# Second attention of a two-layer network: score matmuls in two 64-row halves of TensorE, and a new order of work

## The reference

```
x   = layernorm(features)             # context, 512 rows per batch
lat = layernorm(latents)              # the residual stream, 512 rows per batch
q   = (lat @ Wq) per head * SCALE     # 16 heads of width 64
kv_input = concatenate([x, lat])      # 1024 keys per batch
k, v = kv_input @ Wk, kv_input @ Wv   # per head
sim = q k^T
sim = sim - max(sim, axis=-1)         # over all 1024 keys, masked ones too
sim = where(kv_mask, sim, -inf)
out = softmax(sim) v
return out @ Wo
```

## Time and profile before

| | us |
|---|---|
| median of 3 runs (3788.44 to 3791.84) | 3791.21 |
| the profiled execution | 3788.78 |
| its span, first to last instruction | 3787.2 |

### The profile page before, as it was taken

The page is one execution under the profiler, slowest core; times in us unless marked ns, Lnnn a source line. Parts: engine busy times, 40 slices in busy tenths (PEclk is TensorE's granted clock), DMA queues, the critical chain, the costliest instruction groups (busy, mean ns, idle before and its releaser), DMA issues. The chain is left out here.

```text
span 3787.2 us, 53181 instructions
## 1 busy us (share of the span) xinstructions
PE 3371.4 (89%) x15933; PEld 2357.3 (62%) x15934; DVE 2206.8 (58%) x4093; ACT 1735.0 (46%) x2612; POOL 1603.3 (42%) x937
## 2 busy tenths in 40 slices
PE   5876999996279999999999999999999975879988
PEld 4655888885246565656565655656556654657766
DVE  5665555555636666666666666666666664212225
ACT  2332333332336666666666666666666642212222
POOL 4012333333125555555555555555555543800037
PEclk8986999998579999999999999999999986989999
DMA  4000000001710100000101001001000021242223
GB/s 102 0 1 13 13 12 12 11 9 67 270 70 18 56 17 33 39 33 17 56 17 56 17 33 42 30 27 46 32 40 34 1 74 51 76 135 62 62 67 107
DMA packets 81015, 176.12 MB, mean 47 GB/s; under 512 B 12000, under 2 KB 57384, under 8 KB 74800
## 3 DMA queue, kind: packets, MB, share of 16 engines
q1 hardware_dynamic: 64896, 136.08, 10.2%
q0 software_dynamic: 11392, 27.36, 2.3%
q10 hardware_dynamic: 4656, 11.80, 0.9%
HBM read 120.83 MB, written 54.30 MB: 46 GB/s over the span
## 5 line engine op out<-in xcount | busy, mean ns | idle before, releaser
L2012 POOL TENSOR_TENSOR d_acc<-d_acc,d_pr 128x1024 f32<-128x1024 f32 x384 | 925.9, 2411 | 192.5 <-ACT d_pr L1920 172.9
L1954 DVE TENSOR_REDUCE d_nm<-d_pS 128x1 f32<-128x512 f32 x1024 | 670.6, 687 | 307.8 <-PE d_pS L1815 299.4
L1920 ACT ACTIVATE d_pr<-d_pT 128x1024 f32<-128x1024 f32 x512 | 506.8, 1023 | 85.8 <-PE d_pT L1838 77.8
L1768 PE MATMUL d_pO<-d_pr,d_V 128*64 128x512 f32 x2048 | 509.3, 608 | 0.0
L2012 POOL TENSOR_TENSOR d_acc<-d_pr 128x1024 f32<-128x1024 f32 x64 | 154.1, 2407 | 771.1 <-ACT d_pr L1920 771.1
L1836 PE MATMUL d_pT<-d_Q,d_K 128*128 128x512 f32 x1024 | 408.2, 399 | 19.4 <-ACT d_pr L1920 18.5
L1815 PE MATMUL d_pS<-d_K,d_Q 128*128 128x512 f32 x1024 | 395.8, 438 | 9.8 <-issue 4.4
L1838 PE MATMUL d_pT<-d_Q,d_K 128*128 128x512 f32 x1024 | 400.4, 391 | 0.0
L1759 PE MATMUL d_pm<-d_kv,d_W 128*128 128x512 f32 x1152 | 314.9, 409 | 62.4 <-ACT d_rb L1913 25.6
L909 POOL TENSOR_TENSOR e_hs<-e_hf,e_hs 128x512 fp32r<-128x512 f32 x136 | 175.6, 1291 | 365.2 <-ACT e_hs L886 365.2
L1815 PEld LDWEIGHTS d_pS<-d_K,d_Q 128*128 128x128 f32 x1024 | 184.7, 190 | 211.1 <-DVE d_nm L1954 125.4
(11 more groups left out here) (282 smaller groups left out, 5328.2 us busy)
## 6 DMA issues: line engine op xcount, KB each, us to landing
d_W<-w_split SPq DMA_DIRECT2D x32, 1536.0 KB, 6.3
kv_split<-c_ys SPq DMA_DIRECT2D x16, 1024.0 KB, 6.5
d_kv<-kv_split SPq DMA_DIRECT2D x8, 2048.0 KB
x_slots<-m_zeros SPq DMA_DIRECT2D x1, 9088.0 KB, 29.8
b_x<-x_slots SPq DMA_DIRECT2D x71, 128.0 KB
y_slots<-b_y SPq DMA_DIRECT2D x71, 128.0 KB
w_split<-c_wq POOLq DMA_DIRECT2D x4, 1536.0 KB, 8.2
b_wgu<-in_r_gu_dram ACTq DMA_DIRECT2D x8, 704.0 KB, 9.1
```

The source lines that it names most:

```text
L1768: last = pe.matmul(pO[own[h], :], V[vb][:, s, par * P + h * HD1:par * P + (h + 1) * HD1], pr[:, s % PT, h, :], start=(s == 0), stop=(s == ...
L1920: act.activation(pr[:, n % PT, :, :], pT[n % 2][:, :, :], ACT.Exp).then_inc(exp_done, 1)
L1954: dve.tensor_reduce(nm2[:, j, (1 - h) * TPB + qt, m:m + 1], pS[:, n % 2, :], AX.X, ALU.max, negate=True).then_inc(max_done, 1)
L2012: pool.tensor_tensor(acc[:, q, :, :], a, pr[:, s % PT, :, :], ALU.add).then_inc(acc_done, 1)
```

## The change

All score matmuls contract over 64 rows. Head 0 lies on partitions 0 to 63, head 1 on 64 to 127, in tiles KH, KL, KM, QH, QL, QM (high, low, and mask/max rows); the padded copies and the units c0 to c2 are gone. ST has four terms per head instead of two, S is one unit for both heads (8 units of two matmuls, both banks of `pS`). The mask leaves S: for the first half of the keys VectorE adds it in the maximum (tensor_tensor_reduce, one per head, after a memset of one column), with a mask row spread over all partitions by a new DMA per step; for the second half one reduction takes both heads. M turns all 128 columns and ScalarE alone copies them. High and low parts are written with one instruction of 128 partitions. Both lists have a new order, and the wait for W and kv stands before whichever of Q, K, V comes first.

```
-    """den M r0 Q r1 ST0 ST1 r2 r3 c2 ST2 K0 c0 ST3 PV0 PV1 PV2 ST4 S0 S1 K1 S2 c1 PV3 PV4 S3 ST5 S4 S5 ST6
-       S6 ST7 S7 S8 Y0 S9 PV5 S10 Y1 S11 S12 PV6 S13 S14 PV7 S15 O N""".split(),
-    """den M Q ST0 r0 ST1 K0 ST2 ST3 c2 c0 r1 r2 PV0 PV1 PV2 PV3 r3 K1 ST4 ST5 S0 S1 Y0 S2 c1 ST6 S3 V0 S4
-       ST7 S5 S6 Y1 PV4 S7 S8 V1 S9 PV5 S10 S11 V2 S12 S13 PV6 V3 S14 S15 N PV7 O""".split())
+    """Q M K0 ST0 S0 ST1 ST2 S1 den PV0 r0 r1 PV1 ST3 S2 ST4 ST5 r2 S3 K1 ST6 S4 PV2 r3 PV3 S5 PV4 PV5 PV6 Y0 S6
+       ST7 Y1 S7 PV7 N O""".split(),
+    """V0 M Q ST0 ST1 K0 ST2 S0 ST3 V1 S1 PV0 den PV1 PV2 PV3 r0 r1 r2 S2 K1 ST4 S3 ST5 V2 S4 r3 ST6 ST7 S5 V3 PV4
+       PV5 Y0 S6 PV6 Y1 PV7 O S7 N""".split())
...
# SyncE, at Q: the mask row over all partitions
+                            if not first and not (isinstance(st.g, int) and st.g == 0):
+                                sp.wait_ge(max_done, MAXES * gp - MAXES)
+                            sp.dma_start(masked[j][:, :], mb[bass.ds(bb, 1), 0:S].rearrange("o n -> (o n)"
+                                         ).partition_broadcast(P)).then_inc(mask_in[j], 16)
...
# TensorE, S
-                            if n > 1:
-                                pe.wait_ge(max_done, 17 * gp + n - 1)
-                            pe.matmul(pS[:, n % 2, :], Q0[j][h][:, qt * P:(qt + 1) * P],
-                                      K2[j][h][:, m * S:(m + 1) * S], start=True, stop=True).then_inc(s_done, 1)
+                            if n:
+                                pe.wait_ge(max_done, MAXES * gp + maxes_before(n))
+                            for h in range(2):
+                                last = pe.matmul(pS[:, h, :], QH[j][own[h], qt * P:(qt + 1) * P],
+                                                 KH[j][own[h], m * S:(m + 1) * S], start=True, stop=True)
+                            last.then_inc(s_done, 1)
...
# TensorE, ST
-                            for h in range(2):
-                                pe.matmul(pT[s % 2][:, h, :], K1[q][h][:, s * P:(s + 1) * P], Q1[q][h][:, :],
-                                          start=True, stop=False)
-                                last = pe.matmul(pT[s % 2][:, h, :], K2[q][h][:, s * P:(s + 1) * P], Q2[q][h][:, :],
-                                                 start=False, stop=True)
+                            terms = [(KM[q], QM), (KL[q], QH[q]), (KH[q], QL[q]), (KH[q], QH[q])]
+                            for i, (k_, q_) in enumerate(terms):
+                                for h in range(2):
+                                    last = pe.matmul(pT[s % 2][:, h, :], k_[own[h], s * P:(s + 1) * P],
+                                                     q_[own[h], :], start=(i == 0), stop=(i == len(terms) - 1))
...
# VectorE, S (m is the half of the keys)
-                            dve.tensor_reduce(nm2[:, j, (1 - h) * TPB + qt, m:m + 1], pS[:, n % 2, :], AX.X,
-                                              ALU.max, negate=True).then_inc(max_done, 1)
+                            if m == 0:
+                                for h in range(2):
...
+                                    dve.memset(turn[:, h:h + 1], 0.0)
+                                    dve.tensor_tensor_reduce(biased[:, h, :], pS[:, h, :], masked[j][:, :], -1.0,
+                                                             MASKED, ALU.add, ALU.min,
+                                                             nm2[:, j, h * TPB + qt, m:m + 1]).then_inc(max_done, 1)
+                            else:
+                                both = nm2[:, j, :, m].rearrange("p (o t) -> p o t", o=2)[:, :, qt]
+                                dve.tensor_reduce(both, pS[:, :, :], AX.X, ALU.max, negate=True).then_inc(max_done, 1)
```

More of the change, by code:

```diff
@@ L1590, in order @@
     if isinstance(st.g, int) and st.g == -1:
-        return ([(u, 0) for u in PROLOGUE] + [("c", c) for c in (2, 0, 1)] +
-                [("S", c) for c in range(4 * TPB)] + [("N", 0)])
+        return ([(u, 0) for u in PROLOGUE] +
+                [("S", c) for c in range(2 * TPB)] + [("N", 0)])
     uses = uses_of(st)
@@ L1641, in layer1_pairs @@
         W = [sb(f"d_W{k}", [P, 2, 3, DC, 256], F32R) for k in range(2)]
-        K1, K2 = ([[sb(f"d_{n}{j}{h}", [P, KEYS], F32R) for h in range(2)] for j in range(2)] for n in ("K1", "K2"))
-        Q0, Q1, Q2 = ([[sb(f"d_{n}{j}{h}", [P, S], F32R) for h in range(2)] for j in range(2)]
-                      for n in ("Q0", "Q1", "Q2"))
+        KH, KL, KM = ([sb(f"d_{n}{j}", [P, KEYS], F32R) for j in range(2)] for n in ("KH", "KL", "KM"))
+        QH, QL = ([sb(f"d_{n}{j}", [P, S], F32R) for j in range(2)] for n in ("QH", "QL"))
+        QM = sb("d_QM", [P, S], F32R)
+        masked = [sb(f"d_masked{j}", [P, S]) for j in range(2)]
+        biased = sb("d_biased", [P, 2, S])
+        turn = sb("d_turn", [P, 2])
         V = [sb(f"d_V{k}", [P, NKT, 256]) for k in range(2)]
@@ L1771, in outputs @@
                         last.then_inc(pv_done, 1)
+                    first_use = next((u for u in uses_of(st) if u[0] in "QKV"), None)
                     if not first:
@@ L1776, in emit @@
                     for what, n in order(st):
+                        if not first and st.off in (1, 3) and what == first_use:
+                            pe.wait_ge(w_in[wk], 16 * (2 * st.b + st.batch_half) + (16 if st.off == 1 else 32))
+                            if st.off == 3:
+                                pe.wait_ge(kv_in, 16 * (st.b + st.batch_half + 1))
                         if what in ("K0", "K1"):
@@ L1819, in emit @@
                                 pe.wait_ge(wo_in, 16)
[L1820 removed]
+                                pe.wait_ge(set_rows, 4 * 16)
+                            pe.wait_ge(max_done, MAXES * st.g + MAXES)
                             for qt in range(TPB):
[L1822 removed]
+                                last = pe.matmul(pS[:, 0, qt * P:(qt + 1) * P], nm[:, q, qt, :],
                                                  identr[:, :], start=True, stop=True)
@@ L1878, in emit @@
                             act.wait_ge(misc_done, use(st, what))
-                            for h in range(2):
-                                act.copy(K1[j][h][own[h], i * S:(i + 1) * S], pm[own[h], :]).then_inc(k_hi, 1)
-                        elif what == "c" and n < 2:
-                            half = slice(n * S, (n + 1) * S)
-                            for h in range(2):
-                                act.wait_ge(k_hi, 4 * gp + 2 * n + h + 1)
-                                act.copy(K2[j][h][own[h], half], K1[j][h][own[h], half].bitcast(F32)
-                                         ).then_inc(copied, 1)
+                            act.copy(KH[j][:, i * S:(i + 1) * S], pm[:, :]).then_inc(k_hi, 1)
                         elif what == "Q":
@@ L1890, in emit @@
                                 act.wait_ge(st_done, NKT * st.g)
-                            for h in range(2):
-                                act.mul(Q1[j][h][own[h], :], pm[own[h], :], SCALE1).then_inc(q_hi, 1)
-                        elif what == "c":
-                            for q_, rows in ((Q0, own), (Q1, other)):
-                                for h in range(2):
-                                    act.wait_ge(q_hi, 2 * gp + h + 1)
-                                    act.copy(q_[j][h][rows[h], :], Q1[j][h][own[h], :].bitcast(F32)).then_inc(copied, 1)
+                            act.mul(QH[j][:, :], pm[:, :], SCALE1).then_inc(q_hi, 1)
                         elif what[0] == "V":
@@ L1986, in _ @@
                 for j in range(2):
-                    for h in range(2):
-                        for b_ in (K2, Q0, Q2):
-                            pool.memset(b_[j][h][:, :].bitcast(F32), 0.0).then_inc(set_up, 1)
+                    pool.memset(KM[j][:, :].bitcast(F32), 0.0).then_inc(set_up, 1)
                 pool.memset(onerow[:, :].bitcast(F32), 1.0).then_inc(set_up, 1)
@@ L1992, in _ @@
                 pool.memset(ones[:, :], 1.0).then_inc(set_up, 1)
+                pool.wait_ge(set_up, SET_UP - 2)
+                for c in (1, HD1 + 1):
+                    pool.memset(nm[:, :, :, c:c + 1].bitcast(F32), 1.0).then_inc(set_up, 1)
                 pool.memset(ahead[:, 6:7], 0.0).then_inc(pv_done, PT)
```

84 lines of the change are left out of this document (36 added, 48 removed).

## The result

The changed kernel takes 3731.49 us (median of 4 runs, 3729.24 to 3735.42); the kernel before, run beside it, 3790.93. The ratio is 0.9845 [0.9828, 0.9862]: 1.5% faster, where 3733 had been forecast. The profiled execution took 3729.24 us, its span 3727.4.

A forecast was written before the change was run, and what follows sets the result against it. TensorE was taken as the bound (97% busy in the steps). Slots, shape changes, stalls and loads gave a 60.8 us period against 62.64; 1.84 x 31.5 = 58 us off 3788.8 is 3731, median 3733, range 3650 to 3880.

The forecast's parts named there:

- Fewer S, in pairs: TensorE's S slots fall from 32 to 16 per period if the row halves run side by side: -3.64 us.
- 0.3 us for loads of a pair: Two 128-column weight loads per row pair instead of one, 80 pairs: up to 0.7 us a period, 0.3 taken.
- Changes of shape: TensorE switching between full, rows and columns, 34 times a period at 0.20 or 0.14 us: 6.3 against 3.7, +2.6.
- Stalls of the new lists: TensorE waits per period: K0 behind M 1.2, Q behind V0 0.65, ST2 and ST5 0.25 each; 2.35 us in all.
- S in lockstep doesn't hold TensorE: S waits for both heads' maxima, about 2.1 or 1.8 us, within the lists' margins; rival of slower VectorE, chance 0.09.
- The mask DMA: 256 KB broadcast issued at Q, 0.6 us at 434 GB/s, needed about 3.5 us later at S0: nearly 3 us room.
- The period: Den to next den but one, a step without V and one with: 62.64 to 60.8 us, 1.84 saved.
- The walk: Unit-by-unit timing of the new lists: step without V 27.45 us, with V 33.2; 60.7, with loads 60.8.
- Off the path: ScalarE's 16 copies per period (9.9 us), half the 64-partition writes, one row copy go: worth only shorter waits already walked.
- Prologue: Before the steps: 4.4 us of copies go, a serial S chain of 15.8 replaces 16 reductions: about zero, within 3 us.

The follow-up runs named there:

- e1: Changed kernel with both score matmuls of an S reading the same upper 64 partitions, so they cannot run side by side: 3834.66 us, ratio 1.0119.
- e9: Changed kernel with two more shape changes per period, Y0 moved between PV5 and PV6, V3 between ST6 and ST7: 3742.94 us, ratio 0.9873.
- e3: Changed kernel with the mask left out of the maximum, one reduction for both heads everywhere: 3729.67 us, ratio 0.9839.
- e4: Changed kernel with the biased maximum (tensor_tensor_reduce) computed twice per head: 3916.53 us, ratio 1.0335.
- e2: Changed kernel with the old lists, every second S struck out and no copies: 3871.85 us, ratio 1.0217.
- e5: Changed kernel with ScalarE doing the 8 removed 64x512 copies again, into a tile nobody reads: 3743.87 us, ratio 0.9875.
- e6: Changed kernel with another order, M Q ST0 ST1 K0 in the step without V and S moved later in both lists: 3708.17 us, ratio 0.9783.
- e11: The e6 kernel run once more beside the changed kernel on one chip: 3709.61 us, ratio 0.9787.
- e7: Kernel before the change with the new lists, two old S units for each new one and its copies kept: 4129.71 us, ratio 1.0897.
- e8: Changed kernel with two more shape changes per period, Y0 moved between PV4 and PV5, V3 between ST6 and ST7: 3761.25 us, ratio 0.9919.

## Why the prediction was right, point by point

- *Fewer S, in pairs.* -3.64 us forecast. The two matmuls of a pair start mostly 3 to 4 ns apart (a few up to 10) and pairs follow at 0.23 us, and e1, which takes the overlap from S alone, gives back 3.17. The 0.3 us for loads of a pair is not seen.
- *Changes of shape.* 34 at 0.17 to 0.20, forecast +2.6 over before. By e9 0.34 for two, 0.17 each, where the forecast's mean was 6.3 / 34 = 0.185. Right as a price of one more change. Over the whole period more is left, by an estimate: 61.18 less 51.6 of slots (55.2 less 3.64) and 2.4 of stalls is 7.2 us, where the forecast had 6.3 for the changes and 0.3 for the loads.
- *Stalls of the new lists.* K0 behind M 1.23 (forecast 1.2), Q behind V0 0.67 (0.65), ST2 and ST5 0.23 each (0.25). Right, but for what stands behind them, see the period below. K0 stood 3.07 us after Q, as walked, and ST0 4.65.
- *S in lockstep doesn't hold TensorE.* Right, shown by e3 (nothing gained by a cheaper maximum) and e4 (5.85 lost by a dearer one). The lists are what makes it so, as e2 shows.
- *The mask DMA.* This term was mis-sized: I had "0.6 us and nearly 3 us of room". Where S0's maximum waited for the row, it came 3.23 to 3.65 us after its issue. And the issue is late. SyncE's queue waits for the high part of Q in every step, and two small DMAs of mask rows stand ahead of the broadcast (the rows at 1455.81 and 1456.55), so it is issued 3.06 us after Q's start, about 3 us before S0 can be reduced:

```profile
SPq L1718 <- ACT d_QH L1892: 896.7, 40, 29.6
```

It costs next to nothing all the same. In the step shown den starts 8.56 us after Q; in one other it is 8.50, and in the remaining 18 without V, waiting for the mask or not, 8.40 to 8.42. That is 0.15 us in the worst step and about 0.01 a period.
- *The period.* The walk missed 0.38 us in the step without V (27.83 against 27.45) and 0.15 in the other; 0.15 of that was covered by the 0.3 for loads less rounding. The 0.38 is there by S3, 14.58 us after Q against 14.2 walked. ST2 and ST5 stand behind a wait, and from each to the S after it TensorE takes 1.03 us, in all 20 periods, where the walk had the plain 0.91: the first pair behind a wait is as long as the one behind a change of shape. These two places are 0.25 of the 0.38. The walk put its 0.11 "for the exposed load" ahead of the start only.
- *Off the path.* 0.45 us a period for the copies, not nothing (e5).
- *Prologue.* This was a term mis-sized, and it hid the miss of the period. From the first projection to the first ST: 49.94 us before, 40.23 after, -9.7, where I had 0 within 3.

The sum of the parts: the spans of the two profiled executions, 3787.2 and 3727.4, are 59.8 us apart. Up to the first ST 6.0 (that 9.7 less 3.7 by which the load of W came later), from the first ST to the last den 50.0, behind it 3.8, which lies in phases that were not touched. The forecast had 58 for the middle and 0 for the two others. So the total is right to 2 us because a gain of the middle that was 8 us too large met 9.8 us from elsewhere; that the total came out so close is luck. The step that failed in size is the period: 1.84 us forecast, 1.46 measured, of which 31.5 make 46 of the middle's 50; the other 4 are at its ends. The 3.7 and the 3.8 are about as large as what differs anyway: the first projection starts between 1049 and 1057 us in the profiled executions (1049.1 in e6 and 1056.7 in e11, which are one kernel), and behind the last den the eleven experiments, with the same work there, have 692.8 to 696.4 us, where the kernel before has 697.6 and the changed one 693.8.

Where the prologue's gain comes from: its windows, before and then after (columns as in the earlier trace rows; the clock is the third from the end):

```profile
1054.00:1064.00 10.00, 5.81 (x13) 3.60 (x13) 2.76 (x4) 2.32 (x4) 0.00 (x0) 0.50 0.70 263
1064.00:1077.70 13.70, 11.66 (x48) 10.49 (x48) 0.00 (x0) 1.75 (x3) 0.00 (x0) 0.50 0.00 1
```

```profile
1056.90:1063.00 6.10, 3.31 (x12) 2.10 (x12) 1.38 (x2) 1.17 (x2) 0.00 (x0) 1.00 0.77 319
1063.00:1071.80 8.80, 6.76 (x50) 6.02 (x50) 0.00 (x0) 1.75 (x3) 0.00 (x0) 1.00 0.01 2
```

K and V ran at a granted 0.50, that is 1.2 GHz, before, and at 1.00, 2.4 GHz, after. The same work, in which a gap for the copies was 2.1 us before and is 1.4 now. The V part alone is 13.7 against 8.8 us. That the shorter gaps raised the clock is likely and not shown. Eleven profiled executions have the gaps of 1.4 us, and in ten of them the clock is 1.00 from the second projection on; in e7, with the gaps of 2.1, the projections ran at 0.50 as before. The eleventh is e11: its K and first V ran at the lower clock all the same (starts 4.32 us apart in place of 3.06), though it is the same kernel as e6, which had the upper one. From the first projection to the first ST e6 took 39.7 us and e11 43.6. So this part of the gain can fail to come in another execution of the same kernel. The S part of the prologue in turn is longer, 15.1 us from the first S to the next projection against 14.0, about as forecast for the chain; but the 4.4 us of copies ahead of it are gone, as forecast too. TensorE has one pair there and then waits for its maximum, and the clock falls again:

```profile
1077.50:1088.00 10.50, 5.01 (x13) 2.39 (x14) 5.98 (x10) 0.00 (x0) 0.00 (x0) 0.50 0.00 0
```

What stays open: the rest of the period's miss, in small differences along the walk, what delays S4 in e5, and what sets the clock in the prologue.

## What to carry to other kernels

Scores of 64 channels for two heads fit into two row halves of TensorE at the price of one, and the gain is real only if the order of work is rewritten with it: here the form alone lost 4.7% of a period, the order alone 17% (about 7 of it through a clock that fell behind long waits), both together won 2.3%. A long wait can cost twice: once by itself, and once by the lower clock behind it, so read the granted clock of a slow version before you explain its time. Each change between full, rows and columns costs about 0.17 us here, a price to be set against the stall that it would cover: three changes for a 1.2 us stall were worth it. When a forecast total comes out right, add up the stretches of the trace all the same; two errors of opposite sign look like none.

## What the runs showed of the hardware that I had not expected

- Two 64-row matmuls into two banks of PSUM cost one slot of 0.23 us with nothing lost, though both write 128 partitions at once; and a change between full and rows costs as much as one with columns.
- A tensor_tensor_reduce over 512 elements shows as a custom instruction of 688 ns and an accumulator read of 83; memset, instruction and read overlap, two in a row taking 1.32 us.
- The broadcast of one mask row into 128 partitions, 256 KB, was usable 3.23 to 3.65 us after its issue in the 12 steps that waited for it; the rate of 434 GB/s in the earlier trace rows would have it at 0.6.
- Scaling the output, 512 elements with two inputs from SBUF, took 1.41 us in the rows of e8 where I had reckoned with the 0.69 of the earlier trace rows. The groups of the changed kernel have it so all through; the kernel before had 1.14 us already (the same group there, L1974: 73.0 us for 64), which I had not read:

```profile
L1972 DVE TENSOR_TENSOR d_OT<-d_osb,d_rb 128x512 f32<-128x512 f32 x64 | 88.3, 1379 | 2.2
```

- The granted clock in the prologue differs between two executions of one kernel (e6 and e11). In e7 it fell to 0.50 behind waits of up to 3.8 us in the middle of the steps; in the prologue a V of 12 matmuls took 3.6 us from start to start at 0.50 and 2.4 at 1.00.
